# Cross-attention on one core: the mixing product's three terms stacked along its depth in two blocks

## What is computed

```python
text_p  = x @ W_text + b_text            # x: (4, 2048, 512)
audio_p = ctx @ W_audio + b_audio        # ctx: (4, 77, 384)
Q = layer_norm(text_p, g1, beta1);  K = layer_norm(audio_p, g2, beta2);  V = audio_p
alpha = softmax(Q @ K.T / sqrt(512))     # (4, 2048, 77)
H = (alpha @ V) @ W_out + b_out
out = layer_norm(H + x, g_out, beta_out) # (4, 2048, 512)
```

## Time and profile before

| | |
|---|---|
| median of 3 runs (lowest to highest) | 293.68 us (293.34 to 295.71) |
| the profiled execution's own time | 293.24 us |
| its span in the trace | 291.5 us |
| busy share: PE, PEld, DVE, ACT, POOL | 95%, 85%, 81%, 64%, 71% |
| granted clock of the PE, mean | 0.98 of full |
| share of the chain that ended last: PE | 84% |
| of it the lines `project` L1062, `mix` L1075, `transpose_x` L995 | 40%, 15%, 9% |

### The profile page before, as it was taken

How to read it: one execution, slowest core, us unless ns; L and a number is a source line. 1 busy time by engine, 2 the same in 40 slices (tenths; PEclk the granted TensorE clock), 3 DMA queues, 4 the chain that set the end, 5 groups by cost and what they waited for, 6 DMA issues and landing times.

```text
span 291.5 us, 6254 instructions
## 1 busy us (share of the span) xinstructions
PE 275.9 (95%) x1735; PEld 248.9 (85%) x1735; DVE 236.3 (81%) x665; ACT 187.8 (64%) x467; POOL 208.1 (71%) x227
## 2 busy tenths in 40 slices
PE   7799999999999999999999999999999999999850
PEld 7579759989999999999999999999999999999740
DVE  2299866688888898888888888888888889888864
ACT  3574335246777777777777777777777777777650
POOL 5084400111688898889888888898888889888864
PEclk9999999999999999999999999999999999999975
DMA  6819790321244344444443444344434444441115
GB/s 186 313 53 302 282 305 0 116 89 66 76 152 148 145 145 144 145 144 144 144 144 144 148 152 159 141 150 157 172 141 165 155 143 146 150 144 72 74 72 216
DMA packets 20659, 43.31 MB, mean 149 GB/s; under 512 B 2035, under 2 KB 4671, under 8 KB 20647
## 3 DMA queue, kind: packets, MB, share of 16 engines
q1 hardware_dynamic: 20023, 42.11, 41.7%
q10 hardware_dynamic: 624, 1.06, 1.3%
HBM read 21.19 MB, written 16.78 MB: 130 GB/s over the span
## 4 chain that ended last, share of the span: by engine, by line
PE 84%; DMA 4%; POOL 4%; SPq 4%; issue 1%; DVE 1%; ACT 1%; POOLq 0%; ACTq 0%
PE psY L1062 40%; PE psO L1075 15%; PE psT L995 9%; PE psY L1052 7%; DMA wa<-in_L_xattn_W_audio_dram 3%; SPq L303 3%; PE psE L1038 2%; PE psY L970 2%; PE psY L1015 2%; PE psY L899 1%; PE psT L970 1%; DMA val_lo<-zs 1%; POOL vT_lo L356 1%; POOL zs L436 1%; POOL zs L440 1%
## 5 line engine op out<-in xcount | busy, mean ns | idle before, releaser
L1062 PE MATMUL psY<-proj_hi,x_hi 128*128 128x464 f32 (+3 forms) x256 | 85.8, 335 | 0.0
L1062 PE MATMUL psY<-proj_hi,x_lo 128*128 128x464 f32 (+3 forms) x256 | 82.9, 324 | 0.0
L1062 PE MATMUL psY<-proj_lo,x_hi 128*128 128x464 f32 (+3 forms) x256 | 82.9, 324 | 0.0
L399 POOL TENSOR_TENSOR zs<-zs,shift 128x512 f32<-128x512 f32 x56 | 72.2, 1289 | 4.4
L393 POOL TENSOR_TENSOR zs<-zs,gain 128x512 f32<-128x512 f32 x56 | 72.4, 1292 | 1.0 <-ACT zs L566 1.0
L405 POOL TENSOR_TENSOR rstd<-stat_eps,neg_half 128x4 f32<-128x4 f32 x31 | 31.5, 1017 | 51.7 <-DVE stat_eps L785 51.7
L536 ACT ACTIVATE x_hi<-psT 128x512 fp32r<-128x512 f32 x64 | 38.4, 600 | 41.3 <-PE psT L995 41.3
L555 ACT ACTIVATE waste_act<-hid,sc 128x512 bf16<-128x512 f32 x64 | 45.9, 717 | 6.3 <-DVE hid L793 4.2
L1062 PEld LDWEIGHTS psY<-proj_hi,x_lo 128*128 128x128 f32 x256 | 48.3, 189 | 1.5
L684 DVE TENSOR_TENSOR x_lo<-psT,x_hi 128x512 fp32r<-128x512 f32 x64 | 44.2, 691 | 6.1 <-ACT x_hi L536 3.9
L1062 PEld LDWEIGHTS psY<-proj_hi,x_hi 128*128 128x128 f32 x256 | 48.5, 189 | 0.7
(11 more groups left out here) (213 smaller groups left out, 490.9 us busy)
## 6 DMA issues: line engine op xcount, KB each, us to landing
xs<-in_x_dram SPq DMA_DIRECT2D x64, 256.0 KB, 3.0
out_dram<-zs SPq DMA_DIRECT2D x29, 512.0 KB, 3.8
out_dram<-zs SPq DMA_DIRECT2D x6, 256.0 KB, 2.0
xs<-in_L_xattn_W_text_dram SPq DMA_DIRECT2D x4, 256.0 KB, 4.6
xs<-in_L_xattn_W_out_dram SPq DMA_DIRECT2D x2, 512.0 KB, 10.3
wa<-in_L_xattn_W_audio_dram SPq DMA_DIRECT2D x1, 768.0 KB, 9.2
proj_hi<-proj_hi SPq DMA_DIRECT2D x1, 768.0 KB, 6.1
proj_lo<-proj_lo SPq DMA_DIRECT2D x1, 768.0 KB, 5.1
```

The costliest lines, as they stand in the source:

```text
L399: nc.gpsimd.tensor_tensor(zs[:, q, t, :], zs[:, q, t, :], shift[:], ALU.add).then_inc(out_ready, 1)
L1062: last = nc.tensor.matmul(psY[:, t, to:to + n0], part[:, par, t, k * P:(k + 1) * P], w[:, q, at:at + n0], start=(n == 0), stop=(n == len(P ...
```

## The change

**The mixing product.** The three terms are stacked along the depth, 3 x 77 = 231 rows, in two blocks of at most 128: block 0 holds the high probabilities (77 rows) and the first 51 of the low ones, against the high values (77) and their first 51 again; block 1 holds the last 26 low ones and the high ones again, against the last 26 high values and the low values (103 rows). `mix` issues two products for three.

**The probabilities.** They are split ahead of their transposes: ACT writes the exponentials to PSUM (the rest of bank `psD`), `prob_round` copies them from there, 154 elements a partition, into the middle of the tile `parts` (columns 26 to 102 of 154, for each t), and DVE's `prob_rest`, now two subtractions of 102 and 52 elements a partition, fills the columns on both sides. `transpose_prob` then transposes two overlapping windows of 128 columns for each t, four transposes for two, waits for `prob_lo_ready`, and fills all of bank `psE`. A new ACT instruction, `parts_out`, copies it (128 x 512) to `parts_t`; `mix` waits for that.

**Order.** ACT: exponentials, `prob_round`, `hi_part` (t=1), `parts_out`. DVE: `prob_rest` stands right behind `scores_and_quad` (t=0), ahead of `residual` (t=1); before, it stood behind `inverse_sum`. At the end, ACT has `prob_round` and `parts_out` ahead of `normalise`.

**The values.** They go to `wo_hi`/`wo_lo` (W_out's halves, read last by `values_product`), in 21 transfers for 12, as soon as `val_psum` has reached 3; `value_hi` and `value_lo` are called before the scores' weights are split and not between.

```diff
-        wtT_hi, wtT_lo = val_hi, val_lo
+        val_a, val_b = wo_hi, wo_lo
@@ SP
-                    sp.wait_ge(m_psum, KD)
+                    sp.wait_ge(val_psum, len(KEYS))
+                    for n in range(len(KEYS)):
+                        sp.wait_ge(val_hi_ready, n + 1)
+                        sp.wait_ge(val_lo_ready, n + 1)
+                        for high, dst, q, row, at, w in segments(n):
+                            src = f32(vb_hi) if high else vbuf
+                            sp.dma_start(f32(dst[row:row + w, q, :]), src[at:at + w, n, :]).then_inc(val_placed, 16)
@@ ACT, preparation
+            value_hi(0)
+            value_hi(1)
             hi_part(0, 0, 0)
+            value_hi(2)
@@ ACT, loop
+                wait_if_positive(act, prob_lo_ready, 1, i, b - 2)
-                    nc.scalar.activation(prob[:, b % 2, t, :], logits[:, b % 2, t, :], ACT.Exp,
+                    nc.scalar.activation(prob[:, t, :], logits[:, b % 2, t, :], ACT.Exp,
             def prob_round(b, i):
+                wait_if_positive(act, prob_ready, T, i, T * (b - 2) + T)
+                wait_if_positive(act, probT_psum, 1, i, b - 2)
+                nc.scalar.activation(parts[:, :, S_B:S_B + S], prob, ACT.Copy).then_inc(prob_hi_ready, 1)
+            def parts_out(b, i):
                 wait_if_positive(act, probT_psum, 1, i, b - 1)
                 wait_if_positive(act, mix_psum, T, i, T * (b - 4) + T)
-                nc.scalar.activation(prob_hi[:, b % 2, :], psE[0:S, 0:T * P], ACT.Copy).then_inc(prob_hi_ready, 1)
+                nc.scalar.activation(parts_t[:, b % 2, :, :, :].rearrange("p t h r -> p (t h r)"), psE[:], ACT.Copy).then_inc(parts_t_ready, 1)
@@ DVE, preparation
             lo_part(0, 0, 0)
+            value_lo(0)
+            value_lo(1)
             lo_part(0, 0, 1)
+            value_lo(2)
@@ DVE, loop
-                nc.vector.tensor_tensor(prob_lo[:, b % 2, :], psE[0:S, 0:T * P], f32(prob_hi[:, b % 2, :]),
+                nc.vector.tensor_tensor(parts[:, :, S_B + S:2 * S], prob[:, :, 0:S_A], f32(parts[:, :, S_B:S_B + S_A]), ALU.subtract)
+                nc.vector.tensor_tensor(parts[:, :, 0:S_B], prob[:, :, S_A:S], f32(parts[:, :, S_B + S_A:S_B + S]),
                                         ALU.subtract).then_inc(prob_lo_ready, 1)
@@ PE
-                wait_if_positive(pe, prob_ready, T, i, T * (b - 2) + T)
-                wait_if_positive(pe, prob_lo_ready, 1, i, b - 2)
+                wait_if_positive(pe, prob_lo_ready, 1, i, b - 1)
+                wait_if_positive(pe, parts_t_ready, 1, i, b - 2)
                 for t in range(T):
-                    last = nc.tensor.transpose(psE[0:S, t * P:(t + 1) * P], prob[:, b % 2, t, :], ident[:])
+                    nc.tensor.transpose(psE[:, 2 * t * P:(2 * t + 1) * P], f32(parts[:, t, S_B:2 * S]), ident[:])
+                    last = nc.tensor.transpose(psE[:, (2 * t + 1) * P:(2 * t + 2) * P], f32(parts[:, t, 0:P]), ident[:])
...
-                wait_if_positive(pe, prob_lo_ready, 1, i, b - lag + 1)
+                wait_if_positive(pe, parts_t_ready, 1, i, b - lag + 1)
-                for n, (pr, v) in enumerate(((prob_hi, val_hi), (prob_hi, val_lo), (prob_lo, val_hi))):
-                    last = nc.tensor.matmul(psO[:] if mixed is None else mixed, pr[:, (b - lag) % 2, t * P:(t + 1) * P], v[0:S, q, :],
-                                            start=(n == 0), stop=(n == 2))
+                for n, (v, rows) in enumerate(((val_a, P), (val_b, S + S_B))):
+                    last = nc.tensor.matmul(psO[:] if mixed is None else mixed, parts_t[0:rows, (b - lag) % 2, t, n, :], v[0:rows, q, :],
+                                            start=(n == 0), stop=(n == 1))
```

More of the change, by code:

```diff
@@ L87, in cross_attention @@
         proj_lo = sb("proj_lo", [P, B, COLS], F32R)
-        val_hi = sb("val_hi", [P, B, H], F32R)
-        val_lo = sb("val_lo", [P, B, H], F32R)
+        wtT_hi = sb("wtT_hi", [P, KH, D], F32R)
+        wtT_lo = sb("wtT_lo", [P, KH, D], F32R)
         score_c = sb("score_c", [P, B, SC])
@@ L106, in cross_attention @@
         neg_max = sb("neg_max", [P, B, T])
-        prob = sb("prob", [P, 2, T, S])
+        S_A = P - S
+        S_B = S - S_A
+        prob = psD[:, BS + 2 * T:BS + 2 * T + T * S].rearrange("p (t s) -> p t s", t=T)
+        parts = sb("parts", [P, T, 2 * S], F32R)
         prob_sum = sb("prob_sum", [P, B, T])
         inv_sum = sb("inv_sum", [P, B, T])
-        prob_hi = sb("prob_hi", [S, 2, T * P], F32R)
-        prob_lo = sb("prob_lo", [S, 2, T * P], F32R)
+        parts_t = sb("parts_t", [P, 2, T, 2, P], F32R)
         hid = sb("hid", [P, 2, T, H])
@@ L165, in cross_attention @@
         assert KH * D == B * H
-        wtT_hi, wtT_lo = val_hi, val_lo
+        assert KH == B
+        val_a, val_b = wo_hi, wo_lo
         wt_loaded = [sem(f"wt_loaded{k}") for k in range(KD)]
@@ L216, in cross_attention @@
         prob_hi_ready, prob_lo_ready = sem("prob_hi_ready"), sem("prob_lo_ready")
+        parts_t_ready = sem("parts_t_ready")
         mix_psum, hid_ready, sq_ready = sem("mix_psum"), sem("hid_ready"), sem("sq_ready")
@@ L223, in cross_attention, with segments @@
         gain_p_ready, shift_p_ready, early_gain, gained_ready, out_tail = sem("gain_p_ready"), sem("shift_p_ready"), sem("early_gain"), sem("gained_ready"), sem("out_tail")
-        SEGMENTS = sum(1 for at, w in KEYS for q in range(B) if max(q * S, at) < min((q + 1) * S, at + w))
+        PLACES = ((True, val_a, 0, 0, S), (True, val_a, S, 0, S_A), (True, val_b, 0, S_A, S), (False, val_b, S_B, 0, S))
+        def segments(n):
+            at, w = KEYS[n]
+            for high, dst, row, first, last in PLACES:
+                for q in range(B):
+                    lo, hi = max(q * S + first, at), min(q * S + last, at + w)
+                    if lo < hi:
+                        yield high, dst, q, row + lo - q * S - first, lo - at, hi - lo
+        SEGMENTS = sum(1 for n in range(len(KEYS)) for _ in segments(n))
         f32 = lambda ap: ap.bitcast(F32)
@@ L546, in _ @@
                                      M_BANK[k][:, 0:BS].rearrange("p (b s) -> p b s", b=B), ACT.Copy).then_inc(m_hi, 1)
-                if k < len(KEYS):
-                    value_hi(k)
             def square(b, i, t):
@@ L595, in body @@
                     exponentials(b, i)
+                    prob_round(b, i)
                 if live(0):
@@ L598, in body @@
                 if live(2):
-                    prob_round(b, i)
+                    parts_out(b, i)
                 if live(3):
@@ L617, in _ @@
             prob_round(1, END)
+            parts_out(1, END)
             normalise(1, END, 0)
@@ L757, in _ @@
                     link(nc.vector.memset(floor, H * EPS))
-                if k < len(KEYS):
-                    value_lo(k)
             dve.wait_ge(cd_ready, 1)
@@ L828, in body @@
                     scores_and_quad(b, i, 0)
+                if live(2):
+                    prob_rest(b, i)
                 if live(3):
@@ L838, in body @@
                         nc.vector.tensor_tensor(zs[:, b, 0, :], zs[:, b, 0, :], GAIN_P, ALU.mult).then_inc(early_gain, 1)
-                    prob_rest(b, i)
                 if live(1):
```

3 lines of the change are left out of this document (1 added, 2 removed).

## The result

The changed kernel takes 290.77 us in the median of 20 runs (288.92 to 293.61), the kernel before 292.4 us in 20 runs beside them (290.98 to 295.9). The ratio is 0.995, with a 95% interval of 0.9927 to 0.9973: faster by 1.6 us, about half of one per cent. The forecast was 290.9 us for the median, in a range of 286.4 to 296.8; the gain forecast was 2.8 us, the gain measured 1.6 us. The profiled execution after has a span of 289.1 us (own time 290.86) against 291.5 us (293.24) before.

The account below looks back on a forecast made before the run. The PE bounded the loop at 7.06 us a step; afterwards the path from scores back to scores would, at 6.95. Loop -3.1, preparation -0.1, end +0.4 gave -2.8 us: 290.9 us, range 286.4 to 296.8.

Parts of the forecast that it names:

- The loop, the period: Loop, scores of t=1 from step to step: 7.06 us falls to 6.95, saving 3.1 us over 28 steps.
- way round: Loop, from one step's scores through softmax, split and transposes to the next step's scores: 6.95 us, setting the period.
- The PE's own work: PE in the loop: two `mix` products fewer (-0.48 us), two transposes more (+0.22), 7.06 to 6.80 us a step.
- The terms of the leg: Loop, exponentials' end to `transpose_prob`: ACT's wait 0.03, `prob_round` 0.33, `prob_rest` 0.37, DVE to PE 0.04; 0.77 us.
- The rival by the rule on the DRAIN: Loop, no overlap in `prob_rest`: 0.45 us, period 7.03, 0.8 us saved; part of no gain (293.3 to 295 us), chance 0.15.
- Preparation: Before the loop: 21 value transfers issued 41.4 to 57.6 us, first `mix` not held by them; gain 0.1 us.
- The end: the mis-sized term: After the loop: last `transpose_prob` 0.24 us sooner, but `normalise` at 280.4 for 279.96: 0.4 us lost.
- The sum: Whole kernel: loop -3.1, preparation -0.1, end +0.4, together -2.8 us, giving a median of 290.9 us.
- The PE stays the bound: Loop rival: other engines' path only 6.80 us, so the PE sets the period; -7.0 us, 286.7 us, chance 0.25.
- Slower through the split's leg: Loop rival: exponentials' end to `transpose_prob` above 0.88 us, up to 1.0; period 7.18, +3.7, 297.4 us, chance 0.20.

Follow-up runs that it names:

- tp_two_later: Changed kernel with `transpose_prob` put behind eight products of `project` (t=1) instead of six: 287.12 us, ratio 0.9802 to the kernel before.
- best: Changed kernel with its loop written out, `transpose_prob` two products later and, at the end, `normalise` ahead of `parts_out`: 285.65 us, ratio 0.9768 to the kernel before.
- before_unrolled: Kernel before with its loop written out for all steps, so no body restarts the loop's code: 292.26 us, ratio 1.0015 to the kernel before.
- after_padded: Changed kernel with a useless ACT copy of 77 elements between the maximum and the first exponential: 294.88 us, ratio 1.0078 to the kernel before.
- before_padded: Kernel before with a useless ACT copy of 77 elements between the maximum and the first exponential: 292.05 us, ratio 0.9985 to the kernel before.
- only_values_early: Kernel before with only the values' new placement: 12 transfers into W_out's halves, splits called sooner: 292.48 us, ratio 0.9989 to the kernel before.
- before_same_edits: Kernel before with its loop written out and, at the end, `normalise` ahead of `prob_round`: 292.34 us, ratio 1.0011 to the kernel before.

## Why the prediction was right, step by step

**The loop, the period.** Forecast 6.95, measured 6.96; forecast saved 3.1 us, measured 2.7; the 0.01 us between the periods is 0.3 over 28 steps. The number was right for a reason that was only half right. The sum had one mean value, 1.16, for scores to `residual` in three kinds of bodies, and came to one way round of 6.95 for all. In truth that way is 6.85 in the two short bodies, level with the PE, 7.21 in the body that restarts the loop and 6.99 in the one behind it. A mean over bodies gave the right sum only because the way round is nowhere shorter than the PE's own work. With 0.1 us less in every body the two short ones would have stayed at the PE's 6.84, and the mean would have promised more than came.

**The PE's own work.** Forecast 6.80, measured 6.84 (the short steps of tp_two_later, all of best). The two products that went had cost 0.24 us each, as said, and depth cost nothing: in the loop the products 128 and 103 deep are busy for 409 and 397 ns, those 77 deep were for 413 and 397. The four transposes were through in 0.37 us (179.03 to 179.40), so two more cost 0.24 and not 0.22; the other 0.02 lies within the rounding of the rows.

**The terms of the leg.** `prob_round` 0.30 us (forecast 0.30); the two parts of `prob_rest` 264 and 202 ns busy, started 0.18 apart and through in 0.38 (0.37); ACT's wait for its own exponentials 0.03 to 0.04 (0.03); DVE to PE 0.06 (0.04); transposes to the scores 1.96 to 2.0 (2.01). An exponential into PSUM is busy for 310 ns where it took 347 into SBUF, which I had left at the old price. The way round did not become shorter by it: from the first exponential to the last sum read out it is 0.78 us as before (184.62 to 185.21 and 0.19). The Trainium skill (ScalarE: Activation LUTs, "Step-by-step: what each stage is for") says that ScalarE writes PSUM faster than SBUF; the trace agrees, with 0.037 us for 77 elements. Over the loop ACT has 5.6 us a step (forecast 5.7) and DVE 6.0, where the forecast let it rise from 6.2 to 6.3.

**The rival by the rule on the DRAIN.** By the rule as the prediction put it, the second part of `prob_rest` would have begun 0.26 us behind the first; it began after 0.18 (185.76 to 185.94), and the trace disagrees. The Trainium skill itself (VectorE: DVE Perf Modes, "Two Vector instructions with no wait between them") says that an instruction is held until the one ahead has finished when it reads or writes at another starting group of 32 partitions. These two read and write at the same ones, so by it nothing holds the second. With that the trace agrees, and the prediction should have weighed it beside the other.

**Preparation.** The 21 issues ran from 41.87 to 57.90 us, 0.80 each (forecast 41.4 to 57.6). In the third step the PE waited for the split and not for a transfer, as forecast, and the first `mix` started at once behind `project`:

```profile
60.95 0.33 PE L1063 MATMUL psE<-ident,parts 128*128 128x128 f32 x1 [0.71 <-DVE parts L838]
...
62.74 0.41 PE L1101 MATMUL psO<-wo_hi,parts_t 128*128 128x512 f32 x1
```

The fourth step's scores stand at 69.79 for 69.3. Of that 0.5 us come from the load of W_audio, which landed after 9.7 us where it took 9.2 before, ahead of everything the change touches; without it, 69.3. So the -0.1 us of this part is worked out and was not measured: in tp_two_later the same load took 8.8 us, and the start of one execution differs from that of the next by more than this term.

**The end: the mis-sized term.** Forecast +0.4 us, measured +1.4 at like clock. This is the term of the sum that was wrong. The step of the prediction that failed is the one that let the last `transpose_prob` start 0.24 us sooner, at 278.76. Two things were missed. The step after the last full one has no transposes of x: before, it took the PE 6.22 us, and the way round, which the change had made the limit, does not get shorter with it (6.86): +0.64. And the last `transpose_prob` waits 0.37 us for `prob_rest`, 4.80 us behind the scores where it stood 4.52 before: +0.28. From the start of the transposes to that of the copy behind them it is 0.69 us for 0.41: +0.28. The 0.5 us between `parts_out` and `normalise` was as forecast (277.07 to 277.57), 0.22 more than before. Together 1.42: `normalise` starts 12.85 us behind the last full scores for 11.43. The forecast had the last two of these four (0.44 at half clock, and 0.22), less a start that it took to be sooner (0.24). In best, with `normalise` ahead of the copy, the end is as long as before_unrolled's (23.04 and 23.01).

**The sum.** -2.7 - 0.1 + 1.4 = -1.4 us by the parts at like clock; the medians say -1.6. The forecast 290.9 came out all the same, and by luck: it was set against a median of 3 runs, 293.68, that lies 1.3 us above that of 20, and this makes up for the 1.2 us by which the gain was forecast too large.

**The rivals.** "The PE stays the bound" gives 28 x (7.058 - 6.84) = 6.1 us in the loop; it is what best does (tp_two_later, at 6.88, does 4.9 of it), and it missed in the changed kernel by the restart (2.9 us) and by under 0.02 us a step besides (0.5 us). "Slower through the split's leg": from the last sum read out (184.62 + 0.78) to `transpose_prob` (186.20) the leg took 0.80 us in the body shown, near the forecast's 0.77 and below the 0.88 from which the period would be longer than before. after_padded shows how near that was: with 0.15 us more the kernel is slower than before.

## What to carry to other kernels

An engine that is busy all the time hides how long the way round through the others is; before work is taken from it, add that way up body by body, with the body that restarts the loop apart, and compare each with the engine's own work: the period is the mean of the larger of the two, not the larger of the two means. A wait put into the middle of a row of products has two windows, what is ahead of it and what is behind it, and moving it by two products gave nearly as much again in the 28 steps (2.2 us) as the change itself (2.7). Where a step at the end of a loop is short of some work, ask whether the new limit gets shorter with it.

## What was not expected of the hardware

**In the last 20 us the clock falls earlier in some executions than in others.** The same 16 passes took 1.95 us in eleven of the fourteen profiles, after, before_unrolled and before_padded among them, and 3.24 to 3.57 us in before, only_values_early and before_same_edits; the last two digits of the clock row are 95 or 85 there and 75 here. In before the granted clock is 0.50 from 277 to 279 us and 1.00 again by 280; in before_unrolled it stays at 1.00 to 280.9. Ahead of them the PE had worked through the loop and then waited for `residual` (1.27 us in before, 1.28 in before_unrolled), so the rows ahead of them do not tell the two apart. Over 25 executions of the kernel before, run beside each other, the 12 with a mean granted clock of 0.985 and more have a median of 291.71 us, the 9 at 0.979 to 0.981 one of 293.13: 1.42 us apart, as the two ends in the table are 1.45. That the two groups are these two ends is inferred from this, since the kernel before has one profile. The other four, at 0.974 and less, took 295.2 to 296.7 us; no profile shows one of these. The Trainium skill (TensorE: Matmul & The Clock Gate, "Part 1: The HAM clock gate") says that the same kernel runs a different number of its first products at the low clock from run to run; the traces here show such a difference at the end of the kernel.

**A restart of the loop costs the DVE some 0.3 us, and its next body 0.15.** From the scores to `residual` the DVE takes 1.34 us in the body that starts the code anew and 1.05 in the short ones (180.99 to 182.33, 167.29 to 168.34). In the body behind the restart it takes 1.20 (188.20 to 189.40), and that is the 0.14 us by which this body is long. The kernel before has the same three values, where they lie off the path; with the loop written out there is only the short one. What holds the DVE there, the traces do not say. On ACT the restart is the smaller part: `residual` to `square` is 0.86 us (182.33 to 183.19) for 0.78.
